# Scatters and gathers in two of three slots, sparse tiles first in the tail, and a weight's split one slot later

## What is computed

```python
# attention: 16 heads of 8 features
logits = einsum('bhqd,bhkd->bhqk', Q, K) / sqrt(8)
attn = sin(30.0 * logits)
x = x + einsum('bsd,ed->bse', einsum('bhqk,bhkd->bhqd', attn, V), Wo) + bo
# mixture: one shared expert for all tokens, and the best 2 of 8 for each token
x = layernorm(x)
out = expert(x, shared)                      # silu(x @ Wg.T) * (x @ Wu.T) @ Wd.T
scores, idx = top_k(sigmoid(x @ Wr.T + rb), 2)
for e in range(8): out = out + cw[..., e:e + 1] * expert(x, e)
```

## Time and profile before

| | |
|---|---|
| median of 3 runs | 527.17 us (526.96 to 528.3) |
| profiled execution | 527.88 us, its span 526.1 us |
| TensorE busy | 440.0 us (84%) |
| ScalarE busy | 352.7 us (67%) |
| VectorE busy | 287.4 us (55%) |
| GpSimd busy | 244.1 us (46%) |
| granted TensorE clock, mean | 0.948 |

### The profile page before, as it was taken

The page is one execution under the profiler, slowest core; times in us unless marked ns, Lnnn a source line. Parts: engine busy times, 40 slices in busy tenths (PEclk is TensorE's granted clock), DMA queues, the critical chain, the costliest instruction groups (busy, mean ns, idle before and its releaser), DMA issues.

```text
span 526.1 us, 13124 instructions
## 1 busy us (share of the span) xinstructions
PE 440.0 (84%) x4648; PEld 232.1 (44%) x4648; DVE 287.4 (55%) x1039; ACT 352.7 (67%) x559; POOL 244.1 (46%) x333
## 2 busy tenths in 40 slices
PE   3889799899867999999898989988877989439773
PEld 1222134233212445545443454444435889329672
DVE  5956373345423546585634666745365774218765
ACT  2688789988838986887666767876673567216341
POOL 4533431201770233248867422287778556740711
PEclk9999999999987999999999899999999999759967
DMA  5058479174036524732378247421223233311211
GB/s 155 1 142 213 113 217 327 32 210 92 32 116 172 104 62 142 185 72 77 111 205 143 66 127 187 95 65 39 72 56 101 72 87 89 85 41 39 61 32 31
DMA packets 82480, 56.12 MB, mean 107 GB/s; under 512 B 29040, under 2 KB 76784, under 8 KB 82416
## 3 DMA queue, kind: packets, MB, share of 16 engines
q1 hardware_dynamic: 78112, 47.74, 35.2%
q0 software_dynamic: 3584, 7.35, 5.3%
q10 hardware_dynamic: 720, 0.20, 0.2%
HBM read 22.62 MB, written 27.13 MB: 95 GB/s over the span
## 4 chain that ended last, share of the span: by engine, by line
PE 56%; issue 14%; DVE 10%; ACT 8%; POOL 4%; another core or an unknown queue 4%; DMA 2%; SPq 1%; ACTq 0%; DVEq 0%; POOLq 0%
PE o_ps L646 14%; PE score L633 8%; ACT attn L883 5%; PE g_ps L757 4%; PE g_ps L755 4%; PE g_ps L756 3%; PE d_ps L773 3%; DVE hid L1188 2%; PE d_ps L775 2%; PE score L756 2%; PE d_ps L774 2%; PE score L755 2%; DVE x_all L1231 2%; PE score L757 2%
## 5 line engine op out<-in xcount | busy, mean ns | idle before, releaser
L883 ACT ACTIVATE attn<-score 128x1024 f32<-128x1024 f32 x256 | 249.2, 1026 | 31.0 <-PE score L633 23.9
L1393 POOL TENSOR_TENSOR hid_lo<-hid,hid_hi 128x256 f16<-128x256 f32 x119 | 81.5, 687 | 188.8 <-DVE hid_hi L1195 140.0
L646 PE MATMUL o_ps<-attn,vals 128*32 128x512 f32 x1024 | 140.9, 614 | 1.6 <-ACT o_t L890 1.4
L633 PE MATMUL score<-queries,keys 64*128 64x512 f16 x512 | 84.0, 386 | 15.6 <-ACT attn L883 12.2
L1188 DVE SCALAR_TENSOR_TENSOR hid<-g_ps,gate 128x256 f32<-128x256 f32 x102 | 43.1, 422 | 83.6 <-ACT gate L904 69.1
L904 ACT ACTIVATE gate<-g_ps 128x256 f32<-128x256 f32 x102 | 39.3, 386 | 65.6 <-PE g_ps L757 44.0
L755 PE MATMUL g_ps<-xt,w_hi 128*128 128x128 f16 x272 | 49.7, 221 | 6.0 <-DVE hid L1188 3.9
L756 PE MATMUL g_ps<-xt,w_hi 128*128 128x128 f16 x272 | 49.6, 220 | 4.1 <-issue 4.1
L757 PE MATMUL g_ps<-xt,w_lo 128*128 128x128 f16 x272 | 49.5, 220 | 2.0 <-issue 2.0
L773 PEld LDWEIGHTS d_ps<-w_hi,hid_hi 128*128 128x128 f16 x200 | 19.7, 99 | 65.4 <-issue 55.1
L773 PE MATMUL d_ps<-w_hi,hid_hi 128*128 (+1 forms) x200 | 40.4, 226 | 7.2 <-issue 3.4
(11 more groups left out here) (215 smaller groups left out, 987.2 us busy)
## 6 DMA issues: line engine op xcount, KB each, us to landing
y_sorted<-y_sb SPq DMA_DIRECT2D x84, 64.0 KB
q_four<-q_parts SPq DMA_DIRECT2D x14, 256.0 KB
queries<-q_four SPq DMA_DIRECT2D x14, 256.0 KB
k_four<-k_minus SPq DMA_DIRECT2D x14, 256.0 KB
keys<-k_four SPq DMA_DIRECT2D x14, 256.0 KB
x_sorted<-zeros SPq DMA_DIRECT2D x2, 1472.0 KB, 10.8
queries<-q_three SPq DMA_DIRECT2D x14, 192.0 KB
keys<-k_three SPq DMA_DIRECT2D x14, 192.0 KB
```

The source lines that it names most:

```text
L633: mm = pe.matmul(score[h][:, i, :], keys[b % 2][rows, 2 * j + h, kt * P:(kt + 1) * P], queries[b % 2][rows, 2 * j + h, :], start=True, sto ...
L646: mm = pe.matmul(o_ps[32 * i:32 * i + 32, :], vals[b % 2][:, kt, h:h + 32], attn[k % RING][:, i, :], start=(k == 0), stop=(k == UNITS - 1))
L883: act.activation(attn[k % RING][:, 2 * (u % 2):2 * (u % 2) + 2, :], score[u % 2][:, :, :], ACT.Sin, scale=SIN_SCALE).then_inc(sined, 1)
L1393: pool.tensor_tensor(hid_lo[i % HB][:, :], hid[i % HR][:, :], hid_hi[i % HB][:, :], ALU.subtract).then_inc(lo_by_pool, 1)
```

## The change

Four edits of the schedule, and no other work:

- scatter k stands k + k//2 slots behind the first, in place of k, so that two of three slots hold one. The slots of gathers are chosen so that no three in a row hold scatters or gathers. What depends on these slots moves with them: the sparse tiles of groups 0 to 2 begin 8 slots later (123, 187 and 251, before 115, 179 and 243). Of group 1's 16 gathers 12 now stand in the tail (slots 263 to 279; one before). Group 2's stand in slots 288 to 310 (before 291 to 306), group 3's in 312 to 322 (before 313 to 320).
- in the tail a sparse tile that is ready goes first. Slots 256 to 290 hold 35 sparse tiles without a break, 291 to 295 the last shared ones, 296 to 327 the 32 full ones. Before, every third slot went to a shared or full tile while sparse ones were left, and the last tile stood in slot 326. The tail has 72 tiles, before 71.
- `split_weights` stands one slot later on VectorE.
- `stage_weights` for the expert after next stands one slot later on SyncE.

```diff
 def scatter_slot(g, k):
-    return SLOTS * (ROUTE_GROUPS[g][-1] + 1) + S_SCATTER + k
+
+    return SLOTS * (ROUTE_GROUPS[g][-1] + 1) + S_SCATTER + k + k // 2
...
         ready = sparse and sparse[0][0] <= a
 
-        other = not ready or (a - TAIL) % 3 == 0
+        other = not ready
...
         a, mine = Y_SLOT[LAST_RANK[g]] + 6, []
         while len(mine) < SCATTERS[g]:
-            if a not in taken:
+            near = [a + d in taken for d in (-2, -1, 0, 1, 2)]
+            if not (near[2] or near[0] and near[1] or near[1] and near[3] or near[3] and near[4]):
                 mine.append(a)
                 taken.add(a)
             a += 1
...
-                e = prep_at(a - 2)
+                e = prep_at(a - 3)
                 if e is not None and e + 2 < EXP:
                     stage_weights(e + 2)
...
-                e = prep_at(a - 1)
+                e = prep_at(a - 2)
                 if e is not None:
                     split_weights(e)
```

More of the change, by code:

```diff
@@ L269, in scatters_at @@
     return [(g, k // (2 * TT), k // 2 % TT, k % 2) for g in range(len(ROUTE_GROUPS))
-            for k in [a - scatter_slot(g, 0)] if 0 <= k < SCATTERS[g]]
+            for k in range(SCATTERS[g]) if scatter_slot(g, k) == a]
 def gathers_at(a):
```

## The result

The changed kernel takes 495.48 us (median of 4 runs, 494.78 to 497.93), the kernel before 527.2 on the same chip (526.96 to 528.3). The ratio is 0.9416, 95% interval 0.9378 to 0.9454. The forecast was 494. The direction and the largest term held, but that the total is met so closely is luck: two terms of the sum, row 3 and the tail's opening, were off by 7.9 and 5.6 us in opposite directions, and part of the explanation was missing. The experiments, in four further groups, show what it was. The expectations also call it a trickle.

The account below looks back on a forecast made before the run. No engine was full; GpSimd's long runs of indirect DMAs were taken to make other engines trickle. 527.88 - 2.2 + 0 - 9 + 0.5 - 3.5 - 28.6 + 8 + 1.2 = 494.3, stated as 494 us; range 481 to 514.

Parts of the forecast that it names:

- the tail's opening: Start of the tail: 35 sparse tiles in a row at SyncE's pace, 1.15 us each; -3.5 us, bounds -6.5 and +4.
- The cause of the crawl: Tail stretches where engines start instructions late: caused by GpSimd's long runs of indirect DMAs, run length mattering; 28.6 us lost.
- the crawl has another cause: Rival for the tail: the crawl moves or stays, only the split's gain is left; about 526 us, chance 0.04.
- the calm stretch: Tail stretch with 12 silus in 12.0 us, so 1.0 us a tile; against it two stretches lose 28.6 us.
- The split: Start of a row: xn ahead of VectorE's later split removes ScalarE's sine idle of 2.62 us; -2.2, bounds -2.6 and 0.
- Row 3's scatters: Attention row 3: shorter scatter runs leave the 8.7 us loss in place; 0, bounds -4 and +2.
- Rows 4 to 7: Attention: runs of four gathers go in rows 5 to 7, -9, bounds -13 and -4; one tile leaves, -0.5.
- six gather pairs at 0.45: Tail's opening: its share of the tail's 18 gather pairs, each costing 0.45 us; all 18 priced at +8.
- The pairs behind it: Tail after its opening: the other 12 of 18 gather pairs, 0.45 us each; all 18 +8, from 0 to 3 each.
- The crawl and what stands behind slot 290: Later tail: runs of 16 and 8 gathers become pairs, -28.6; 12 pairs, GpSimd's pace +1.2 and one more tile +1.0.
- The rest of the schedule: Tail behind slot 290: GpSimd's pace over 12 periods, +1.2, and one tile more, +1.0.
- pairs are dear in the tail: Rival: at 1 to 2.2 us each, the tail's 18 pairs cost 18 to 40; 504 to 525 us, chance 0.17.

Follow-up runs that it names:

- the packed kernel: Whole change with the gathers of the last two groups packed again, one in each slot from 288 to 311: 515.3 us, ratio 0.9760 to the kernel before.
- chip C: Chip of the second experiments, without the crawl: kernel before 483.1 us; whole change 476.2 us, ratio 0.9867; slots and split with old tail order 468.5 us.
- chip A: Chip of the main result, with the crawl: kernel before 527.2 us, whole change 495.48 us, ratio 0.9416.
- the kernel with later loads: Kernel before with scatters still packed, but sorted tiles' loads, sparse tiles and what follows moved to where spaced scatters put them: 475.3 us, ratio 0.9881.
- chip E: Chip of the fourth experiments, with the crawl: kernel before 525.8 us; whole change with packed tail gathers 515.3 us; slots and split with old tail order 489.1 us.
- chip B: Chip of the first experiments: kernel before 482.5 us; slots alone 469.8 us, order of the tail alone 486.5 us, split and staging alone 480.8 us.
- chips C and D: Chips without the crawl; kernel before 483.1 and 483.0 us. Slots and split with old tail order: ratio 0.9711; the same with packed tail gathers: 0.9775.
- the best version: New slots and split one slot later, with the old order of the tail, against the kernel before: 468.5 us, ratio 0.9711, on chip C; 489.1 us, 0.9256, on chip E.

## Why the prediction came out right

**The cause of the crawl: held, with a condition.** The forecast said that the length of a run is what matters. Breaking the runs of 16 and 8 brought the 13.84 and 6.51 us of the earlier trace rows down to 2.33 and less, and packing them again cost 18 us. The rival "the crawl has another cause" is out for the chips that have it. That it depends on the chip was not seen, and could not be from one trace. The span difference of the tail between chips A and C, 28.1 us, is near the 28.6 that the calm stretch had given. Two things stay open. Breaking a run also makes it slower, two gathers in 3.1 us or more where a run has two in 2.5, and no run here tells length from rate. And what GpSimd's indirect DMAs and the other engines share is not shown. The gathers and silus themselves last as long on chip A as on C; what grows is the time before them.

The Trainium skill's rule that PE and ACT never wait on anyone (SBUF — State Buffer, "Who interferes with whom") speaks of memory ports. Used as a bound on what a DMA can do to another engine's instructions, it would have given 526 for the change and no loss for the packed kernel, which lost 18.

**The split: right.** -2.2 forecast; row 1 went from 40.9 to 38.9 (and began 0.8 us later).

**Row 3's scatters: this step failed.** It said that "the 8.7 us lost in row 3 stay: 0", with a bound of -4. Row 3 went from 51.1 to 43.2, -7.9; it was 11.3 us longer than row 2, not 8.7, and is now 3.4 longer. The step looked only at the crawl and at GpSimd's order. It overlooked that the same edit moves the sorted tiles' load from slot 108 to 116 on SyncE's queue, past the queries' load (slot 12 of the row) and the keys' store (14). The kernel before on chip C shows 5.3 us of row 3's loss without any crawl, and 3.7 go by moving that load alone. On chip A the two causes lie over each other. There SyncE too issued nothing from 148.3 to 158.87 in the kernel before, and one of two stalls of ScalarE of about 4 us is gone behind the shorter runs; the other is the 3.67 above. The row still takes 3.0 us more than on chip C. How the 7.9 divide between queue and shorter runs there isn't settled, since the kernel with later loads ran only where there is no crawl.

**Rows 4 to 7: right in sum, within 2.** -9.5 with the tile that leaves them, measured 210.7 to 199.4, -11.3. Row 5 is at 49.0 and row 7 at 45.3, not near 51, and row 6 takes up part of it. The queue's share was missing here too: on chip C row 5 falls from 51.0 to 48.6.

**The tail's opening: this step failed too.** -3.5 and six gather pairs at 0.45, so -0.8. Measured from the end of the attention to slot 290's silu: 48.5 to 53.3 us, +4.8. (The silus of slots 256 to 290 alone go from 44.2 to 51.0, +6.8, but what stands before them, with the stall of 3.10 us, is 2.0 shorter.) The forecast let the new order gain 3.5 us, since sparse tiles would follow one another at SyncE's pace. On chip C slots 256 to 290 take 46.5 us in the kernel before, 43.0 with the new slots and the old order, and 45.5 with the new order as well. So the slots gain 3.5 there and the order loses 2.5. Chip A takes 5.5 us more than chip C for the changed kernel's opening (51.0 against 45.5); if all of that is the pairs' doing, it is 0.9 for each of the six, twice the 0.45. SyncE was said to be over 90% busy there; it waited 19 of the 51 us for tiles and results, so its queue didn't bind:

```profile
SPq L517 <- PE g_ps L759: 5.9, 3, 3.3
SPq L533 <- ACT y_sb L918: 5.2, 11, 1.4
SPq L517 <- PE score L759: 4.1, 4, 2.2
```

**The pairs behind it: right.** From slot 291 to 327 the changed kernel takes 47.8 us on chip A and 41.5 on C, 6.3 for 12 pairs or 0.53 each, forecast 0.45. With the old order the same stretch takes 47.2 us on chip E and 38.7 on C, 0.7 each. A hid_lo that is late by a stall then delays GpSimd's next pair, so its period is 3.1 to 4.6 us and not 3.1.

**The crawl and what stands behind slot 290:** -28.6, 12 pairs, the pace and one more tile give -21.0; measured from slot 290 to the end 79.4 to 61.9, -17.5. The gap between chips A and C in this part falls from 29.2 to 6.8 us, so the crawl less its pairs gave -22.4, forecast -23.2. The rest of the schedule was priced at +2.2 and costs 4.9 on chip C (50.2 to 55.1), nearly all by the order of the tail: with the old one it is 50.5.

**The sum.** Forecast -33.6: attention -11.7 and tail -21.9. Measured -33.3: -20.5 and -12.8. So 494 was met because the attention gave 9 us more than was counted and the tail 9 less, and nothing in the prediction says that these should cancel. The rival "pairs are dear in the tail", at 1 to 2.2 us each, was nearly true in the opening, at 0.9.

**The order of the tail** was counted as a gain. It is a loss wherever it was measured: 4.0 us alone (chip B), 7.7 on top of the new slots (chip C), and by ratios 0.016 of 526, about 8 us, where the crawl is (chips A and E). Against the old order on chip C the opening takes 2.5 us more (45.5 against 43.0), slots 291 to 327 2.7 (41.5 against 38.8), and the time behind the last silu 2.2. In the second stretch GpSimd doesn't wait behind its first pair and has one pair and hid_lo each 3.26 us (422.46 to 451.79), where the old order has one each 3.1 except behind one wait; the full tiles, with their longer chain on VectorE, stand in one block there. Which of the two makes the 2.7 was only argued: the run meant to tell fell on the chip with the crawl.

## What to carry to other kernels

Break long runs of indirect DMAs on GpSimd with other work: it cost nothing measurable where it wasn't needed (chips C and D) and was worth 18 us of 526 where it was. When an edit moves a slot, list what it is moved past on every queue, SyncE's above all, since a load that waits for a scatter holds everything behind it; moving it from slot 108 to 116, six slots behind the store of the next row's keys, gave about as much as spacing the scatters. And look at the parts apart: here the best version leaves out one of the edits (ratio 0.9256 in place of 0.9416).

## What the runs showed of the hardware

The same program took 526 to 527 us in two of the five groups and 483 in three, 9% apart. The commonest instructions last as long on chip A as on chip C: a sine 1.026 and 1.025 us, a hid_lo 0.687 and 0.697, the matmul of L756 0.220 and 0.221. TensorE's busy time is 440.0 us against 423.2, with a mean granted clock of 0.948 against 0.985; the low clocks on chip A stand in the crawl (0.62 and 0.76 in the earlier trace rows), in which TensorE is mostly idle. Most of the difference is time before instructions. On the slower chips it stands under and just behind GpSimd's indirect DMAs, as stalls of 2 to 14 us that name no releaser, in which TensorE starts a matmul or two and then idles for 1.8 us. A ratio measured on one chip need not hold on another: the whole change is worth 1.3% on chip C and 5.8% on chip A.
